# The weights of the fifth and later experts wait for GpSimd's issue of an add and of its next gather

## What is computed

```python
x = x + 0.5 * ffn(layernorm(x))
x = x + attention(layernorm(x))
x = x + 0.5 * ffn(layernorm(x))
```

```python
probs = softmax(x @ w_router)                       # 32 experts, each token takes its top 4
buf   = zeros(E, CAP, H).at[expert, place].set(x[token])   # at most CAP = 128 tokens an expert
y     = (silu(buf @ w_gate) * (buf @ w_up)) @ w_down       # per expert, F = 176
out   = zeros(T, H).at[token].add(y * weight)
out   = out + sigmoid(x @ w_shared_gate) * ((silu(x @ sw_gate) * (x @ sw_up)) @ sw_down)
```

## Time and profile before

| | us |
|---|---|
| three runs | 939.29, 940.29, 944.42 |
| median | 940.29 |
| the profiled execution, its own time | 938.85 |
| its span, first to last instruction | 937.0 |
| TensorE busy | 909.6 (97% of the span) |
| VectorE busy | 695.9 (74%) |
| ScalarE busy | 531.3 (57%) |
| GpSimd busy | 511.1 (55%) |
| DMA, mean over the span | 109 GB/s |
| loop over the experts, first stage | about 147 to 293 |
| loop over the experts, second stage | about 758 to 905 |

### The profile page before, as it was taken

One profiled execution on the slowest core, in us unless ns is written; L12 is line 12 of the kernel. 1 busy time (PEld: TensorE's weight loads), 2 busy tenths in 40 slices (PEclk: granted clock), 3 DMA queues, 4 the chain that ended last, 5 costly groups with the idle time before them and its releaser, 6 DMA issues.

```text
span 937.0 us, 18000 instructions
## 1 busy us (share of the span) xinstructions
PE 909.6 (97%) x6118; PEld 685.6 (73%) x6118; DVE 695.9 (74%) x1704; ACT 531.3 (57%) x794; POOL 511.1 (55%) x537
## 2 busy tenths in 40 slices
PE   7999999999999999999999999989999999999997
PEld 6878887777778856666666666558788878777786
DVE  6998787555355889989998999988887875544435
ACT  6666743132233478878887888876667531322322
POOL 6343305565553588887888788934432055555530
PEclk9999999999999999999999999999999999999999
DMA  7143247777783610011001002004432377777735
GB/s 260 46 138 109 74 131 183 172 178 174 185 199 59 202 47 24 23 35 32 23 23 41 26 12 79 24 12 131 142 99 73 97 203 173 175 182 177 173 35 178
DMA packets 95512, 101.89 MB, mean 109 GB/s; under 512 B 18768, under 2 KB 86736, under 8 KB 95440
## 3 DMA queue, kind: packets, MB, share of 16 engines
q1 hardware_dynamic: 83152, 83.17, 29.5%
q0 software_dynamic: 12288, 17.83, 11.2%
HBM read 65.44 MB, written 35.54 MB: 108 GB/s over the span
## 4 chain that ended last, share of the span: by engine, by line
PE 63%; DVE 18%; issue 9%; ACT 4%; POOL 4%; DMA 1%; DVEq 0%; POOLq 0%; ACTq 0%
PE zT L1050 7%; PE gu L90 6%; PE gu L92 6%; PE gu L91 6%; PE gu L1070 6%; PE pj_at L90 3%; PE pv_at L1765 3%; PE pj_at L92 3%; PE pj_at L91 3%; PE down L90 3%; PE down L92 3%; PE down L91 3%; PE scores_at L1749 2%; PE zT L1059 2%; DVE turned_at L2007 2%
## 5 line engine op out<-in xcount | busy, mean ns | idle before, releaser
L90 PE MATMUL gu<-x_hi,gu_hi 128*128 128x512 f32 x264 | 120.4, 456 | 0.8 <-DVE act_gu L1353 0.7
L825 POOL DMA_INDIRECT rows<-z_rows,slots x64 | 69.3, 1083 | 67.9 <-DVE slots L1344 48.9
L1867 ACT ACTIVATE capped_at<-scores_at 128x2048 f32<-128x2048 f32 x64 | 93.1, 1454 | 20.5 <-PE scores_at L1749 20.3
L1130 ACT CAST a_hi<-act_gu 128x512 fp32r<-128x512 f32 x96 | 59.2, 617 | 79.1 <-DVE act_gu L1353 65.9
L92 PE MATMUL gu<-x_lo,gu_hi 128*128 128x512 f32 x264 | 103.9, 393 | 0.0
L91 PE MATMUL gu<-x_hi,gu_lo 128*128 128x512 f32 x264 | 103.6, 393 | 0.0
L1875 ACT ACTIVATE probs_at<-capped_at 128x2048 f32<-128x2048 f32 x64 | 95.1, 1487 | 2.5
L90 PE MATMUL down<-down_hi,a_hi 128*128 128x256 f32 x300 | 93.9, 313 | 0.6 <-DVE a_lo L1363 0.4
L1944 POOL TENSOR_SCALAR_AFFINE_SELECT probs_at<-probs_at 128x1024 f32<-128x1024 f32 x64 | 85.5, 1340 | 9.7 <-ACT probs_at L1875 9.0
L1050 PE MATMUL zT<-w_gu,xT 128*128 128x352 f32 x256 | 86.3, 460 | 0.0
L1232 ACT ACTIVATE y<-gu,rows 128x256 f32<-128x256 f32 x64 | 30.3, 473 | 98.5 <-PE gu L1070 89.0
(11 more groups left out here) (262 smaller groups left out, 2603.3 us busy)
## 6 DMA issues: line engine op xcount, KB each, us to landing
w_gu<-in_w_gate SPq DMA_DIRECT2D x64, 176.0 KB, 2.7
w_gu<-in_w_up SPq DMA_DIRECT2D x64, 176.0 KB, 3.3
w_down<-in_w_down SPq DMA_DIRECT2D x64, 176.0 KB
z_rows<-z SPq DMA_DIRECT2D x16, 512.0 KB, 3.6
acc<-base SPq DMA_DIRECT2D x10, 512.0 KB, 3.4
out<-base SPq DMA_DIRECT2D x10, 512.0 KB, 3.3
xn_at<-acc SPq DMA_DIRECT2D x16, 256.0 KB, 2.8
x<-xn_at SPq DMA_DIRECT2D x16, 256.0 KB, 2.1
```

The costliest lines, as they stand in the source:

```text
L90: nc.tensor.matmul(out, w_hi, x_hi, start=first, stop=False)
L825: pool.indirect_dma_start(out=gathered_rows[:, n, :], out_offset=None, in_=m.z_rows, in_offset=bass.IndirectOffsetOnAxis(ap=slots[:, e:e + ...
L1867: nc.scalar.activation(capped[:, u % 2, :, 0:n], scores[:, :, 0:n], ACT.Tanh, scale=QK_SCALE / SOFTCAP).then_inc(capped_ready, 1)
```

## The change

A new semaphore `weights_due` is raised by GpSimd once per expert, at the end of each turn of its loop, that is behind the issue of add(e) and of gather(e + 6) (for e from 26 on there is no gather left). SP waits for it ahead of the request for the gate and up weights of expert e + 4. The waits that were there stay.

```diff
@@ -579,6 +579,7 @@
         y_ready = sem("y_ready", E)
         y_scaled = sem("y_scaled", E)
         added = sem("added", 16 * E)
+        weights_due = sem("weights_due", E)
@@ -784,6 +785,7 @@
                     load_gate_up(e)
                 load_down(e)
             for e in range(HELD_W, E):
+                reached(sp, weights_due, e - HELD_W + 1)
                 reached(sp, gu_done, e - HELD_W + 1)
                 load_gate_up(e)
                 reached(sp, y_ready, e - HELD_W + 1)
@@ -872,6 +874,7 @@
                 add(e)
                 if e + HELD_ROWS < E:
                     gather(e + HELD_ROWS)
+                pool.sem_inc(weights_due, 1)
```

## The result

The changed kernel takes 994.55 us (median of four runs, 992.46 to 995.95) against 941.0 us of the kernel before (four runs, 939.29 to 944.42). The ratio on record is 1.0578, with a 95% interval of 1.0553 to 1.0604; the two medians alone give 1.0569. Forecast were 939.4 us and a range of 936.0 to 944.5: wrong, by 55 us, and on the side of rival C.

A forecast was written before the change was run, and what follows sets the result against it. TensorE was taken to set the time, DMA counting only where late. Loops 0 and holes -0.9 us took the 940.29 us median to 939.4, range 936 to 944.5.

The forecast's parts named there:

- rival C: Expert loops: weights behind the gather slow the adds, TensorE falls to their pace; about 952 us at pace 5.0; chance 0.09.
- the adds' chain: GpSimd in the expert loops: each add waits for the one before; pace under the change taken as 4.3 us.
- the spare of the weights: Expert 4's gate/up request: 9.88 us ahead of use, 3.8 needed, so 6.1 to spare at the loop's start.
- the second part: When weights are requested: expert 4's gate/up request moves from 148.45 to 156.11, 7.66 us later and 9.88 ahead of use.
- the sum had 4.3: Predicted step between adds in the expert loops under the change, in us, under TensorE's 4.50 per expert.
- between 0 and the 0.31: GpSimd's 32 increments per stage: bounds in us for each one's cost, 0.1 taken, covered by the wait for a landing.
- lag: Time from an expert's y being ready to its add's start; forecast near 1 us throughout, against 7.68 at expert 27 before.
- forecast A: Whole kernel: adds keep pace, weights in time, TensorE's hole at the attention shrinks; -0.9 us, 939.4; chance 0.60.
- bounds of 4.0 to 5.3: Limits in us for the adds' pace under the change: 4.0 clear of weights, 5.3 the worst step seen.
- The limit of the lag, 5.9: Late experts: the lag in us past which weights come late, from 7.68 - 0.4 - 1.36.
- my 3.8 for it: Typical time in us a gate/up request needs before use: 0.38 between requests, 3.3 landing, 0.1 semaphore.
- C's formula: Lag at expert 27 for pace p: 0.84 + 12 (p - 4.68) + 15 (p - 4.50); 5.9 reached at p = 4.77.

The follow-up runs named there:

- the memset: Changed kernel with weights_due raised by a small memset on GpSimd behind the gather instead of the increment: 938.16 us, ratio 0.9997 to the kernel before.
- half_weights: Changed kernel, but from the fifth expert on each weight request loads half its bytes (264 KB instead of 528): 938.38 us, ratio 0.9998.
- up_behind: Changed kernel with the up request moved behind the gather (+3.1), gate and down left at +0.3 and +0.7: 941.63 us, ratio 1.0033.
- down_behind: Changed kernel with the down request released by a memset behind the gather (about +3.1), gate and up left near +0.3: 944.29 us, ratio 1.0056.
- inc_before_gather: Changed kernel with the semaphore increment placed between the add and the gather: 959.82 us, ratio 1.0233.

## Why the prediction was wrong

**What bounds the kernel, the adds' chain, the spare of the weights: right.** The chain of adds with one in flight was the right thing to look at, and its pace decided. (Where the prediction sets a landing of 3.8 against steps of 4.79 and 4.90, the like of these steps is the clear step of 4.01.)

**The step that failed** is in the second part: "the request waits until add 0 and gather 6 are issued, at 155.05 + 1.06 = 156.11". I took an increment behind two indirect DMAs in GpSimd's list as one that comes when both are issued. It comes 0.3 us behind the add's start, 2.7 us ahead of that, and so the whole burst falls on the add's own data: the adds' steps were 5.8 us where the sum had 4.3. No row of the trace of before showed when such an increment is raised. The sentence that each increment costs "between 0 and the 0.31" treated it as work of the engine. For an edit that adds a signal, when it is raised is the first thing to bound, and I gave it no bounds.

**What followed from it was right at its own place.** With the memset the kernel is nearly the one that I forecast: request at +3.08 (forecast 3.0), steps of 4.48 behind expert 12, lag 0.8 to 1.1 up to add 28 ("near 1"), Wq at 280.02 (forecast 279.5), the last add at 297.03 (295), the load at 300.74 (299), and TensorE's hole from 1.30 down to 0.27 (0.4):

```profile
307.40 0.50 PE L90 MATMUL gu<-x_hi_third,gu_hi 128*128 128x512 f32 x1 [0.27 <-DVE act_gu L1357]
```

The last add is 2 us later than forecast for a reason that the sum had left out: add 28 starts at 281.09, among the projection weights (requested from 280.02 to 289.8), and lands only after 7.7 us. The lag goes from 0.9 to 4.1, which the end of the stage could just bear. In the kernel before the adds met them too, two adds earlier (a step of 6.17 at add 26).

The span is 936.1 against 937.0, the -0.9 of forecast A. In the medians it can't be told from nothing (938.16 against 938.08), so that the number fits is partly luck.

**Rival C was the right mechanism with too small a price.** I said that a pace of 4.77 decides and priced 5.0 at 952. The mechanism is confirmed (experts pass unharmed until the lag is used up, then TensorE runs at the adds' pace), but its bounds of 4.0 to 5.3 were steps at other places. The limit of the lag, 5.9, belonged to requests behind the gather; from the add's start it is larger. Use lies 165.99 - 152.26 = 13.7 behind the end of `y`; the first wait comes with a lag of 10.5 at add 9, whose weights are requested at 205.48 and used at 208.36, after a wait of 0.27. That is 2.9 from request to use: my 3.8 for it was a little too much. The adds' own pace from add 12 to 26 is 5.82 in the first stage and 5.79 in the second, and with it C's sum over 19 experts gives 19 x (5.82 - 4.49) = 25.3 and 24.7, where 25.7 and 23.7 were lost. With a limit of 10.5 instead of 5.9 the deciding pace of C's formula, by my estimate, is 4.94 instead of 4.77; the kernels with steps of 4.7 to 4.86 (half_weights, up_behind, down_behind) lost nothing inside their loops, and the one at 5.1 (inc_before_gather) lost 4.9 and 7.4 us there.

I gave C 9%, by "weights would have to disturb adds most where they meet them least": true of the place that I assumed. A range that held the unknown of the signal's time would have had to take in the rows' worst step, 5.34, on all experts: about +30 to +40 us by my estimate, and even that is short of the 5.8 that came.

**Missing** in every price was TensorE's clock: it was 0.97 and 0.98 over the loops with their waits, and busy time grew by 8.5 us in the first and 5.8 in the second.

**The two rules of the Trainium skill.** Both stand on the page "DMA: Bandwidth & Descriptors". The Trainium skill's rule to issue a DMA early (section "Rules for kernel authors") would have got the sign right for a reason that the runs don't bear out: requests 5 us before use cost nothing (939.37). With the Trainium skill's taking of turns between queues (section "Queues, rings and completion order") the queue rows agree (27% for the add beside 72% for the weights), but whether it is turn by turn they can't show.

**The end of the first stage.** In down_behind the loops lose nothing (y of expert 31 is scaled at 293.25, before at 293.18), and yet it is 5 us slower. Its last add starts at 301.57 instead of 297.03 with the memset behind the gather, and TensorE's hole at the attention's start is 3.20 instead of 0.27:

```profile
310.38 0.80 PE L90 MATMUL gu<-x_hi_third,gu_hi 128*128 128x512 f32 x1 [3.20 <-DVE act_gu L1360]
```

The hole is 2.9 us longer, and the rest is the clock behind it. For the 5.7 us that follow the hole TensorE gets half of full speed and starts 15 matmuls; with the memset behind the gather it starts 30 in the same 5.7 us:

```profile
310.30:316.00 5.70, 5.62 (x15) 4.55 (x16) 3.67 (x10) 3.29 (x6) 1.68 (x6) 0.50 1.03 332
```

```profile
307.40:313.10 5.70, 5.59 (x30) 4.52 (x31) 3.75 (x9) 4.96 (x9) 1.62 (x6) 1.00 1.04 345
```

The second stage's first y then comes 5.2 us later than with the memset (767.42 against 762.25), the whole difference. So the end of the adds has a price of its own, for which the forecast had looked on the side of the gain alone.

## What to carry to other kernels

A semaphore increment in GpSimd's list said here that the sequencer had got there, not that the work in front of it was issued; to signal "issued", let an instruction of the engine that stands behind it raise the semaphore, and look on the trace at when the waiting side really moves. A wait that releases a burst of transfers ties that burst to one place in another transfer's flight, for every turn of the loop: here it cost nothing where the place was clear, and 55 us where it fell just ahead of the chain's own data. Where a chain of dependent DMAs has little slack, ask for its pace at the very place of the new traffic, and measure it if no row shows it.

## What the runs showed of the hardware

- The `sem_inc` on GpSimd behind two indirect DMAs let SP's request go 0.31 us after the first began its 1.59 us issue; with one indirect DMA in front of it, 0.5 us sooner (-0.2). A memset behind the gather ran at the end of its issue, in 0.11 us, and the request stood at +3.08.
- The landing of an add of 128 rows of 1 KB was 3.8 us with 528 KB of weights requested 1.75 or 3.1 us behind its start, 4.8 with them at -0.2, and 5.5 at +0.3.
- With 352 KB at +0.3 it was 4.3 to 4.4, with 264 KB 4.3: the price isn't even in the bytes, the last third costs most. Among the projection weights it was 7.7.
- In 1.5 us of an add's flight SP's queue held 72% of the engines and GpSimd's 27%, with 59 packets; without weights beside it, GpSimd's moved 144.
- TensorE's granted clock was 0.50 for the 5.7 us behind a hole of 3.20 us and 1.00 from then on; behind a hole of 0.27 it stayed at 1.00. Over a loop with 17.1 us of waits it was 0.97, over the loops before, without waits for weights, 1.00.
